# Twelve transformer sub-layers on one core: the first attention sorted as three batches and one, small loads moved into its block, and TensorE's program of the local layers written out

## The reference, cut to what matters

```python
x = _layernorm(x + _L0_attn_ref(x, L0_attn_Wq, L0_attn_Wk, L0_attn_Wv))
x = _layernorm(x + _L0_xattn_ref(x, ctx_1024, ctx_1024, mask_BxS2_if1, ...))
x = _layernorm(x + _L0_ffn_ref(x, ...))
...
x = _layernorm(x + _L3_ffn_ref(x, ...))      # twelve sub-layers in all
```

## Time and profile before

| | |
|---|---|
| median of 3 runs | 5388.47 us (5385.81 to 5394.13) |
| the profiled execution, its own time | 5394.93 us |
| its span in the trace | 5393.1 us |
| PE's products (matmuls) in the whole span | 45549 |
| first sub-layer, to its last copy of outputs | 0 to 479.18 |
| twelfth sub-layer, from its first product | 3203 to about 5338 |

### The profile page before, as it was taken

How to read it: one execution, slowest core, us unless ns; L and a number is a source line. 1 busy time by engine, 2 the same in 40 slices (tenths; PEclk the granted TensorE clock), 3 DMA queues, 4 the chain that set the end, 5 groups by cost and what they waited for, 6 DMA issues and landing times. The chain is left out here.

```text
span 5393.1 us, 131203 instructions
## 1 busy us (share of the span) xinstructions
PE 4122.7 (76%) x45549; PEld 2416.3 (45%) x45678; DVE 3272.7 (61%) x5912; ACT 2679.9 (50%) x5510; POOL 1336.2 (25%) x2908
## 2 busy tenths in 40 slices
PE   2003767876669896786994679999999999999997
PEld 1002333433332221443441337666666667666765
DVE  7994444544447676435555337676766666666665
ACT  2124623544447575441222436565666566566664
POOL 0062200111101111110000234444444444343443
PEclk7556977988779898887995779999999999999998
DMA  1000020000000000003440000000000000000000
GB/s 33 0 0 3 2 63 28 1 4 1 10 27 1 1 1 1 13 6 101 135 132 4 3 23 28 5 10 23 5 27 5 9 23 5 10 23 6 27 5 11
DMA packets 60379, 110.36 MB, mean 20 GB/s; under 512 B 11351, under 2 KB 43203, under 8 KB 58604
## 3 DMA queue, kind: packets, MB, share of 16 engines
q1 hardware_dynamic: 59126, 101.70, 6.6%
q0 software_dynamic: 784, 1.80, 0.2%
HBM read 96.06 MB, written 1.74 MB: 18 GB/s over the span
## 5 line engine op out<-in xcount | busy, mean ns | idle before, releaser
L673 DVE TENSOR_REDUCE minus_max<-banks 128x1 f32<-128x512 f32 (+4 forms) x1152 | 606.1, 570 | 323.0 <-PE banks L568 316.1
L638 ACT ACTIVATE probs<-banks 128x512 f32<-128x512 f32 (+4 forms) x1152 | 581.0, 556 | 342.0 <-PE banks L606 339.6
L2768 POOL TENSOR_TENSOR loc_cos_part<-loc_cos_part,loc_sin_part 128x512 f32<-128x512 f32 x388 | 494.5, 1275 | 756.3 <-DVE loc_sin_part L3198 756.3
L2841 PE MATMUL banks<-loc_w_qkv,loc_shifted 128*128 (+1 forms) x1552 | 420.0, 417 | 90.9 <-issue 75.9
L2841 PEld LDWEIGHTS banks<-loc_w_qkv,loc_shifted 128*128 128x128 f32 x1552 | 298.3, 202 | 138.9 <-issue 78.3
L606 PE MATMUL banks<-q_stack,k_stack 64*128 64x512 bf16 (+3 forms) x1152 | 255.4, 383 | 101.0 <-DMA q_stack<-max_rows 73.1
L3195 DVE TENSOR_TENSOR loc_cos_part<-banks,loc_table 128x512 f32<-128x512 f32 x388 | 264.6, 682 | 87.1 <-ACT loc_square L3063 86.6
L3231 DVE TENSOR_TENSOR loc_headsT<-banks,loc_sum_inv 128x512 f32<-128x512 f32 x192 | 132.6, 690 | 300.4 <-ACT loc_sum_inv L3103 289.8
L3223 DVE TENSOR_REDUCE loc_minus_max<-banks 128x4 f32<-128x384 f32 x386 | 197.0, 552 | 177.1 <-PE banks L2908 176.4
L697 POOL CAST max_parts<-minus_max 128x8 bf16<-128x8 f32 x192 | 36.7, 191 | 1053.9 <-DVE minus_max L673 1053.9
L3063 ACT ACTIVATE loc_square<-banks 128x512 f32<-128x512 f32 x388 | 226.6, 590 | 142.7 <-PE banks L2841 142.7
(11 more groups left out here) (512 smaller groups left out, 9518.8 us busy)
## 6 DMA issues: line engine op xcount, KB each, us to landing
expert_share<-limited_rows SPq DMA_DIRECT2D x136, 256.0 KB, 4.0
expert_w<-in_L_ffn_pairs_dram SPq DMA_DIRECT2D x84, 192.0 KB, 2.4
loc_w_qkv<-in_L_ffn_Wqkv_dram SPq DMA_DIRECT2D x7, 1536.0 KB, 8.2
expert_share<-grouped_rows SPq DMA_DIRECT2D x32, 256.0 KB, 4.1
q_stack<-max_rows SPq DMA_DIRECT2D x384, 3.0 KB
loc_v_edge<-loc_v SPq DMA_DIRECT2D x192, 32.0 KB, 1.8
fixed_w<-in_L_ffn_experts_dram SPq DMA_DIRECT2D x8, 514.5 KB, 3.7
loc_pack<-in_L_ffn_pack_dram SPq DMA_DIRECT2D x6, 537.5 KB, 4.2
```

Source lines behind the costliest of these rows:

```text
L638: nc.scalar.activation(probs[(a % 2) * C + k][e][0:kn, q0:S], t_bank[e][0:kn, q0:S], ACT.Exp, scale=scale).then_inc(s["exp_done"], 1)
L673: nc.vector.tensor_reduce(minus_max[:, u, e, qs[0]:qs[0] + len(qs)], view, AX.X, ALU.max, negate=True).then_inc(s["max_done"], 1)
L2768: nc.gpsimd.tensor_tensor(cos_part[:, tiles, :], cos_part[:, tiles, :], sin_part[:, tiles, :], ALU.add).then_inc(s["summed"], 1)
L2841: ins = nc.tensor.matmul(g.bank[3 * j][:, (t % 2) * QK:(t % 2 + 1) * QK], xs[:, t * P:(t + 1) * P], w_qkv[:, ds(at, QK)], start=True, stop ...
```

## The change

Four things, none of which touches what is computed.

1. `load_chip` is gone. Its transfers, fills and two small products now stand in the block of the first attention. SP issues first the three weights, the first batch of x transposed and the identity, then the other batches, x and the context. PE waits for the weights and the identity, then for each batch's own part of x transposed. `find_flag` (the sum of |x|) and `store_flag` stand between sorting steps.
2. The sort has groups of three batches (12 tiles) and of one (4 tiles). In the first group the steps of `run` 1, 2 and 4 are done batch by batch as its scores come, the others over 12 tiles at once. All that was done for 8 tiles beside the second group's sort is now done for 12 tiles beside a sort of 4, on the same engines; POOL does the subtractions and additions of these 12. Of the last 4 tiles DVE also does the comparison, and its subtraction and addition are fused with the shift and with the scaling.
3. `place_early` gives the small weights of nine later sub-layers places of their own from the start, and SP loads them all (41 copies with the context) in the first attention's block. Their `load` now only fills, and in `grouped_experts_0` and `fixed_experts_1` it is gone. In `context_attention_2` the mask is still loaded in place, but the projections run before the mask is made.
4. PE's loop over batches 1 to 23 is a Python loop: the 23 batches are written out one after another. The loops of the other engines stay.

```diff
@@ load @@
-            @block.sync
-            def _(sp):
-                for dst, src in copies:
-                    sp.dma_start(dst, src).then_inc(s["loaded"], 16)
-                sp.wait_ge(s["loaded"], 16 * len(copies))
+            if copies:
+                @block.sync
+                def _(sp):
+                    for dst, src in copies:
+                        sp.dma_start(dst, src).then_inc(s["loaded"], 16)
+                    sp.wait_ge(s["loaded"], 16 * len(copies))
@@ context_attention_0, and alike in eight more @@
-        w = {n: sbuf(f"w_{n}", [P, D]) for n in ("q", "k", "v", "o")}
+        w = {n: g.early["context_0", n] for n in "qkvo"}
...
-        load(nc, g, [(w[n][:, :], io[f"L0_xattn_w_{n}"]) for n in w] +
-             [(keep[:, :], io["mask_BxS2_if1"].rearrange("b s -> (b s)").unsqueeze(0))],
-             ones=(rows[:, :, :],), zeros=(key_bias[:, :, :],))
+        load(nc, g, [], ones=(rows[:, :, :],), zeros=(key_bias[:, :, :],))
@@ sorted_attention @@
-    GROUP = 2
-    NG, GT = B // GROUP, GROUP * QT
+    GROUPS = ((0, B - 1), (B - 1, 1))
...
+def sort_order(first, count):
+
+    done = 0
+    for b in range(first, first + count):
+        for done, (run, apart) in enumerate(merging_steps(1, 4)):
+            yield run, apart, done, (b - first) * QT, QT
+    for run, apart in merging_steps(8, S // 2):
+        done += 1
+        yield run, apart, done, 0, count * QT
...
+                sp.dma_start(w["q"][:, :], io["L0_attn_Wq"]).then_inc(s["weights_loaded"], 16)
+                sp.dma_start(g.xT[:, 0:S], io["xT"][:, 0:S]).then_inc(s["xT_loaded0"], 16)
+                sp.dma_start(w["k"][:, :], io["L0_attn_Wk"]).then_inc(s["weights_loaded"], 16)
+                sp.dma_start(w["v"][:, :], io["L0_attn_Wv"]).then_inc(s["weights_loaded"], 16)
+                sp.dma_start(g.ident[:, :], io["c_ident"]).then_inc(s["weights_loaded"], 16)
...
+                for dst, source in copies:
+                    sp.dma_start(dst, source).then_inc(g.early_loaded, 16)
...
+                for b in range(B - 1):
+                    scale_soft(b)
+                    for m in batch_tiles(b):
+                        clip(m)
+                    if b:
+                        back(b - 1)
+                back(B - 2)
+                act.wait_ge(s["max_done"], 2)
...
+                sort(0, {(4, 1, B - 2): find_flag, (32, 1, 0): store_flag})
+                sort(1, {(8, 1, 0): lambda: scans(0), (16, 4, 0): lambda: scans(1), (32, 8, 0): lambda: scans(2),
+                         (64, 1, 0): first_counts, (128, 16, 0): first_sums})
@@ local_attention_layers_3, TensorE @@
-                with nc.Fori(1, BATCHES, engines=(mybir.EngineType.PE,), hint_back_edge=True,
-                             head_slot={mybir.EngineType.PE: 130}) as k:
+                for k in range(1, BATCHES):
                     batch(k, k - 1)
```

More of the change, by code:

```diff
@@ L1769, in sparse_or_soft_attention_0, with merging_steps @@
         y = sbuf("attended", [P, NT, D])
-        load(nc, g, [(w[n][:, :], io[f"L0_attn_W{n}"]) for n in w])
-        sorted_attention(nc, g, w, y)
+        sorted_attention(nc, g, io, copies, w, y)
         finish(nc, g, "tokens", y)
-def merging_steps():
-    run = 1
-    while run < S:
+def merging_steps(first, last):
+    run = first
+    while run <= last:
         apart = run
@@ new lines, in sums, with soft, compared_by @@
+        def sums(m):
+            n = 0 if m < GROUPS[1][0] * QT else 1
+            return turns[n][1][:, m - GROUPS[n][0] * QT, :]
+        def soft(m):
+            return ranked(m) if m < GROUPS[1][0] * QT else turns[0][0][:, m - GROUPS[1][0] * QT, :]
+        def compared_by(n, run, first_tile):
+            before = sum(len(order) for order in ORDERS[:n])
+            at = next(i for i, (r, apart, _, t, _) in enumerate(ORDERS[n]) if (r, apart, t) == (run, run, first_tile))
+            return 2 * (before + at + 1)
@@ L1970, in back @@
+                def back(b):
+                    for m in range(b * QT, (b + 1) * QT):
                         act.wait_ge(s["turned"], m + 1)
@@ new lines, in _ @@
+                pool.wait_ge(g.cast_loaded, 112)
+                pool.wait_ge(s["flagged"], 2)
+                negate_max(0)
+                for b in range(B - 1):
+                    threshold_from(b)
+                    above(b)
+                for b in range(B - 1):
+                    tau_bias(b)
+                for b in range(B - 1):
+                    scale_from(b)
+                    for m in range(b * QT, (b + 1) * QT):
+                        subtract_tau(m)
+                for m in range((B - 1) * QT):
+                    add_soft(m)
@@ L2119, in _, with sort @@
-                n = NG - 1
-                scans(n)
-                inverses(n)
-                for t in range(GT):
-                    subtract_tau(dve, nc.vector, n, t)
-                for t in range(GT):
-                    add_soft(dve, nc.vector, n, t)
+                def sort(n, jobs):
+                    before = 2 * sum(len(order) for order in ORDERS[:n])
+                    for i, (run, apart, done, first, count) in enumerate(ORDERS[n]):
+                        part = first // QT
+                        if not done:
+                            dve.wait_ge(s["scores_copied"], GROUPS[n][0] * QT + first + count)
+                        elif before + i:
+                            dve.wait_ge(s["compared"], before + 2 * i)
+                        if run == 4 and apart == 4:
+                            dve.wait_ge(s["ends_copied"], ends_before(n, 2, part) + 1)
+                        if run > 2 and apart == run // 4:
+                            dve.wait_ge(s["ends_copied"], ends_before(n, run, part) + 1)
+                        compare(n, run, apart, done, first, count)
+                        if (run, apart, part) in jobs:
+                            jobs[run, apart, part]()
```

676 lines of the change are left out of this document (365 added, 311 removed).

## The result

| | before | changed |
|---|---|---|
| median | 5391.3 us (4 runs, 5385.8 to 5394.4) | 5229.7 us (4 runs, 5225.8 to 5232.8) |
| span of the profiled execution | 5393.1 us | 5230.8 us |
| ratio | | 0.9701, 95% interval 0.9684 to 0.9718 |

The account below looks back on a forecast made before the run. DVE's sorting steps bound the first sub-layer's sort, an engine-hopping chain follows, and PE bounds the local layers. 25 + 28 + 110 = 163 us less than the 5388.5 median gives 5225 us; range 5200 to 5268.

Parts of the forecast that it names:

- TensorE's branch: Local layers: without PE's 22 branches back, 75.4 us standing and 29 + 8 half clock go; 110 taken, bounds 75 and 112.
- The others' branches: Local layers: branches of DVE and ACT cost under 0.7 us each and lie hidden beside PE's own work.
- The first rival: Local layers: others' branches make written-out PE wait, or clock stays low; 75 or less of 110 come, about 5260; chance 0.16.
- The loads: Starts of later sub-layers: pauses for small weights go; sum 29 us, 28 taken, bounds 15 and 33.
- The first sub-layer: First sub-layer: the sort ends at 421.1 and the whole at 453.8 in place of 479.2, 25 us less.
- the last chain: First sub-layer, behind the sort: the work on the last four tiles takes 32.7 us, where eight tiles took 55.45.
- Start: First attention: five first transfers land at 6.5, so the sort starts at 17.8, 25.0 us earlier (13 to 27).
- Waits for the ends: First sort: DVE waits 1.5 us, 0 to 6, for ACT to copy batch ends between the next batch's scores.
- More steps and POOL: First sub-layer's sort: twelve more steps cost 4.7 us, and POOL's operations stopping DVE cost 9.2 more.
- The second rival: Second sort: POOL's operations take 3.0 us each whatever DVE does, ending some 25 us after the sort; 5248; chance 0.12.
- the stall that stays: Local layers: PE's fetch stands still at batch edges in any form, so nothing is gained there; 5335; chance 0.05.
- the straight code that is fetched too slowly: Local layers: some 260 instruction packets come late, a loss from 0.63 us each; 5485 at 1 us; chance 0.04.

Follow-up runs that it names:

- experiments two and one: Two: the kernel before with only TensorE's loop written out, 5284.2 us. One: the changed kernel with TensorE's loop put back, 5341.9 us.
- experiment five: Changed kernel with TensorE's batches 2 to 23 in a hardware loop of 11 passes of two batches each: 5241.0 us.
- experiment nine: Changed kernel with the loops over batches and layers of DVE, ScalarE and POOL in the local layers written out too: 5218.8 us.
- experiment eight: Changed kernel with small weights of nine later sub-layers loaded in place again, and the eighth's mask ahead of its projections: 5258.9 us.
- Experiment three: Changed kernel with POOL's seven table transfers issued only after the three weights, the identity and the first part of x transposed landed: 5217.9 us.
- experiment four: Changed kernel with ScalarE copying two scores of the next batch before a batch's first ends, and the values last: 5222.5 us.
- Experiment ten: Changed kernel with POOL's twelve additions and twelve comparisons of the first three batches done on one column of 512 each: 5226.2 us.
- run 2: Not a follow-up run: a sorting step of the first group, done batch by batch; with `apart` 1 it took 1.06 to 1.17 us.
- run 4: Not a follow-up run: a sorting step of the first group, done batch by batch; with `apart` 2 it took 0.69 us.

## Why the prediction was right, step by step

**TensorE's branch: 110 forecast, 110.1 in the traces, 109 and 112 in experiments two and one.** The split was right too: 75.4 us of standing still came out as 72.3 less idle time, 37 us of half clock (29 + 8) as 39.4 less busy time (28.3 + 11.1). What I took for granted, that this is the price of a branch, is not so. It was the price of this loop at this place: 5.1 us here, 3.3 less at another slot, 3 more without note and place, 1.1 for a branch of the loop of two. Had I been asked to shorten the loop and not to remove it, I would have been wrong by 40 us (experiment five).

**The others' branches.** "Under 0.7 us each" and hidden was the weak step. It rested on one branch of DVE, 0.65 us. Another, that of its loop over layers, costs 2.1 us, of which 0.8 reach PE each of the four times. The first rival, that PE written out meets the others, was right as a mechanism and small in size: what it kept back is 10 us, not 35 or more. The 110 did not suffer, since the forecast's upper bound was only 112 and experiment nine finds some 9 us beyond it. The row was the wrong one to rest on: it is the branch of another loop of DVE, and the four stalls of over 2 us stood in the same trace.

**The loads: 28 forecast, 34 in the pair of traces, 29 in experiment eight.** The pauses at the sub-layers' starts moved as forecast. In the third, PE starts 1.75 us after the last copy and not 5.20 (3.45 won, 3.7 forecast); the eighth as a whole is 6.4 us shorter, as forecast. PE's first products there:

```profile
696.06 4.21 PE L1181 MATMUL banks<-early_grouped_router,x_transposed 128*128 128x16 f32 x19 [2.39 <-PEq L69]
```

```profile
2128.32 2.04 PE L360 MATMUL banks<-x_transposed,early_context_q 128*128 128x512 f32 x2 [4.62 <-PEq L1107]
```

The pauses before PE's first product in sub-layers 2 to 7, 9 and 10 are shorter by 21.9 us together, 22.6 forecast. The rest is PE's clock: in the second sub-layer it was granted 0.88 and not 0.83, in the third 0.82 and not 0.78, and these two are 5.3 and 5.9 us shorter where the pauses give 2.5 and 3.5. In the fifth it went the other way (0.79 after 0.81, and the 2.0 us of the pause are lost again). That the shorter pause moved the clock is not shown, and the other traces speak against a fixed effect: with the same pause the third sub-layer was granted 0.78 in five of ten of them and 0.80 or 0.82 in the others. What sets the clock there stays open.

**The first sub-layer: 25 forecast, 18.3 in the pair of traces.** Seven traces whose first sub-layer is this one end it at 472.8 to 477.4, 474.2 in the mean, and two with the old one end it at 492.8 and 495.7; about 20 is the fairer number. The sort ended at 431.95 and not 421.1, 10.8 us late, and the last chain gave 5.1 back. That the forecast of 25 is missed by no more than this is luck in part. Step by step:
- *Start.* 17.8 us and not 25.0: the five transfers landed at 14.2, inside the bounds of 4.5 and 18.06, but I chose 6.5. I had blamed 18.06 on x, its transpose and the context. Experiment three shows that the cause was POOL's 1.8 MB of tables, which start at 1.26 us and which the change left where they were.
- *Waits for the ends.* 7.3 us and not 1.5, outside my bounds of 0 and 6. The estimate looked at how long ScalarE copies, not at what it waits for in between: PE's scores, which in turn wait for ScalarE (experiment four).
- *More steps and POOL.* All DVE sorting instructions are busy for 387.8 us, 12.9 more than before; 4.7 + 9.2 = 13.9 was forecast. Experiment ten gives POOL's prices one by one, and they are the forecast's.
- *Scans.* 15.0 us for twelve and not 13.5: three groups of four, one of them beside POOL's comparisons (5.83 us in place of 4.57).
- *Does POOL keep up?* Its operations shrank to 2.0 to 2.15 us. Subtractions ran from 83.5 to 109 us of the second sort and additions to 135, against 83, 109 and 134. The second rival (3.0 us each) is out, and by experiment ten so is the third (a comparison that holds DVE for all of its time).
- *The last chain.* 27.6 us and not 32.7. The wait for ScalarE was as forecast (4.9 us from the sort's end to the shift, 4.5 forecast); the turning and multiplying took 8.6 and not 11, since half of PE's groups ran at full clock by then.

Of the rivals, the stall that stays and the straight code that is fetched too slowly are refuted: along the straight code PE's waits by "issue" are 5.7 us in six cases, 3.1 of them DVE's branches as above, where the loop had 75.9 at its head alone; and 328 packets are fetched where the loop fetched 367. The Trainium skill, Runtime: NRT & Kernel Launch, "Instruction fetch mechanics", says that sequential fetching is mostly hidden, and that a taken branch breaks it when its target is not in the part that is already there. The traces agree, and add that PE stood 1.4 to 5.1 us at such a branch, by the loop's place and note.

## What to carry to other kernels

A stall at a loop's head depends on the loop's place as much as on the branch; before writing out 23 batches, try another slot or two batches a pass, which here gave 74 and 101 of 112 us. When a few small transfers must come first, look at every queue that starts beside them: large transfers of another engine, started at the same moment, cost 9 us here although the five were first on their own queue. Before a stall is priced from one row, look for the same instruction at every other branch. And when two chains end together, as the sort and the work behind it here, pricing one right (16 us) says nothing of the gain (3 us at most).

## What the runs showed of the hardware that I had not expected

- A loop's price changed by 73.7 us of 5342 with nothing but its first instruction's slot (130 to 20): 3.4 or 1.5 us of stall at each of 22 branches. Why one place is better than another is open: the better place came with 22 fewer packets of instructions, but no run separates the place of the head from that of the branch at the end, nor the note from the place.
- PE ran at full clock after all 32 stalls of 1.25 to 1.8 us (eight products in 1.99 us; slot 20 and two batches a pass). After the 44 of 3.1 to 4.0 us in the kernel before and at slot 130, it did so in 6; in the others the eight took 2.5 to 3.8 us, and which stall was followed by how much did not go by its length. So the last two microseconds of a stall cost more than they last.
- The identity, 64 KB, landed 11.6 us after its issue while seven transfers of POOL's queue ran, and PE could start at 5.2 us, not 14.2, when they came later.
- Two DVE steps of 512 outputs each take different times: that of `run` 2 and `apart` 1 took 1.06 to 1.17 us, that of `run` 4 and `apart` 2 took 0.69, in all three batches of the six traces read for it. They differ in the pattern of the elements; why that matters no run shows. ScalarE copies ends beside the first, but is not the cause: in experiment four it copies beside the second as well, which still takes 0.69. The Trainium skill, SBUF — State Buffer, "Who interferes with whom", lists no port that DVE shares with ScalarE, and the traces agree. The first two rows are the changed kernel's, the last two experiment four's:

```profile
29.79 1.13 ACT L1953 ACTIVATE srt_a<-srt_b 128x1024 f32<-128x1024 f32 x1 [2.31 <-DVE srt_b L2161]
29.79 1.08 DVE L2160 TENSOR_TENSOR srt_a<-srt_b 128x512 f32<-128x512 f32 x1
```

```profile
32.02 1.17 ACT L1955 ACTIVATE srt_a<-srt_b 128x1024 f32<-128x1024 f32 x1 [2.20 <-DVE srt_b L2166]
32.02 0.69 DVE L2165 TENSOR_TENSOR srt_a<-srt_b 128x512 f32<-128x512 f32 x1
```
